# Attention on one core: one PSUM bank for the V product, a ring of three for plain scores and turned maxima, reciprocals and last divisions later

## The chip, the cores and the metric

The kernel runs on one core of a Trainium2 chip. The core has TensorE (PE in the profile, with its weight loads as PEld), VectorE (DVE), ScalarE (ACT), GpSimd (POOL) and a queue that issues DMAs (SP). TensorE writes into PSUM, eight banks of 512 float32 columns on 128 partitions; ScalarE and VectorE read it there. The metric is the device time of one execution in microseconds, median of the runs. The time before is 2050.35 us.

## The reference

One transformer layer on 2048 tokens of width 512, in float32: layer norm, causal attention with 16 heads of 32, an output projection, and a gated feed-forward part whose weights are packed in 4 bits.

```python
qkv = jnp.einsum('bsh,oh->bso', hidden_states, w_qkv)      # 16 heads of 32
scores = jnp.einsum('bhqd,bhkd->bhqk', q, k) * scale
scores = jnp.where(causal, scores, jnp.finfo(scores.dtype).min)
probs = jax.nn.softmax(scores, axis=-1)
attn = jnp.einsum('bhqk,bhkd->bhqd', probs, v)
...
x = x + attention(xn) + feed_forward(xn)
```

## The kernel before

Three stages follow each other: norm and projection, attention, then output projection and feed-forward. Only `attention` is changed. It works on 8 pairs of heads (`p`, heads `a` = 0 and 1).

**What a pair needs.** The queries are four chunks of 512 (`qc`), the keys 16 tiles of 128 (`kt`). A *step* is one chunk with one key tile; the causal mask leaves 4, 8, 12 and 16 of them for the four chunks, 40 in a pair, 320 in all (`STEPS`, `NS`). On the four last tiles of a chunk, the diagonal ones, a step is 512, 384, 256 and 128 columns wide and gets a mask added by a small matmul.

- `scores_t` (L664, mask L669) makes the transposed scores of a step for both heads in `p_st`. The negative row maximum of each query is part of the product: it lies in three rows of `q_stack`.
- ACT takes the exponential of both heads in one instruction, `exps` (L536), into `e_sb`.
- `product_v` (L689) adds a step's product with V into `p_o`, with the sum of the exponentials in an extra column of V. When a chunk is complete, ACT copies it to `o_sb` (`copy_out`, L544) and SP stores it. The sums go through memory and come back as `compact`; `invert_sums` (L592) on DVE inverts them, and POOL multiplies the finished rows later (`normalise`). In the last pair, DVE divides at once from `p_o` (`divide`, L600 and L604).

**Where the row maxima come from.** Plain scores are made one *unit* at a time: `scores` (L634, one matmul of up to 512 columns into `p_s`) and `unit_max` on DVE (L579, on the diagonal L575). There are 80 units in a pair, some 12 groups ahead of their use. When the units of chunk `r` are through, DVE joins them (`join_parts`, L586), POOL splits the maxima into three bfloat16 parts (`split`, L492 to L502), PE turns them into rows (`turn_max`, L651, four matmuls of 128 columns for a head) and ACT copies the rows into `q_stack` (`max_row`, L528). A *turn* here is `turn_max` and its copy for one head.

**Buffers.** `p_st` has two buffers of two banks. `p_s` has two banks in turn: a unit waits until the maximum of the unit two before it is taken (`maxed`). `p_o` has two banks, chunk by chunk, and the turns use partitions 96 to 127 of the same banks.

**Order.** Each engine has its own written-out program, and semaphores join them. A *group* is two steps (`d`, in the changed kernel `k`; 20 in a pair, 160 in all). In a group PE issues: a quarter of the group's units, `scores_t` of the step two ahead, a quarter of the units, `scores_t` of the next one, a quarter, the first head's turn if one is due, `product_v` of both steps, the second head's turn, the last quarter. A group has 6 units at first, 4 from the twelfth on, and none after group 147. ACT does in a group: `copy_out` if a chunk has ended, both exponentials, then the copies of the turns.

## Time and profile before

| | |
|---|---|
| median of 3 runs | 2050.35 us (2049.04 to 2053.05) |
| the profiled execution | 2050.79 us, its span 2049.0 us |
| PE, DVE, ACT, POOL busy | 93%, 54%, 33%, 15% of the span |
| attention | from about 190 to 899.6 us |
| one pair of heads in the middle of attention | about 82 us |

The span is the time from the first to the last instruction; the execution's own time is 1.8 us longer. PE's busy time counts modelled ends of pipelined matmuls, so a busy PE can still be late; the starts of its instructions tell more.

### The profile page before, as it was taken

The page shows a single profiled execution, that of the slowest core. Times are in us where ns is not written, and L with a number is a line of the kernel's source. Part 1 is how long each engine was busy: PE and PEld are TensorE (multiplying, and loading weights), DVE is VectorE, ACT ScalarE, POOL GpSimd, SP SyncE. Part 2 cuts the span into 40 slices and gives each one's busy share as a digit, 9 for nine tenths or more (in the row PEclk, how much of TensorE's full clock was granted, in tenths as well). Part 3 has the DMA queues.
Part 4 walks back from the last instruction along what each step waited for, and adds up shares of the span by engine and source line. Part 5 has one row for each costly group of instructions (what it writes and reads, how often), then busy time and mean ns, then how long its engine had stood idle before and what let it go on. Part 6 is the DMA issues. An engine that isn't in the chain of part 4 may idle for free.

```text
span 2049.0 us, 23233 instructions
## 1 busy us (share of the span) xinstructions
PE 1908.9 (93%) x8448; PEld 1316.4 (64%) x8448; DVE 1098.8 (54%) x1703; ACT 681.7 (33%) x789; POOL 310.2 (15%) x339
## 2 busy tenths in 40 slices
PE   2996899999999999889999999999999999999998
PEld 2785344444444444335777778777877787778776
DVE  7220565555565565533555655655655565556553
ACT  2221244544545455321222222223223223222221
POOL 0002100100110101100222222222122212221221
PEclk9998799999999999999999999999999999999999
DMA  3654504134043040033101110111011101110002
GB/s 143 236 185 129 109 6 91 33 65 85 10 91 76 22 91 6 12 121 124 34 10 31 31 26 4 31 31 31 0 31 31 31 0 31 31 31 0 1 0 83
DMA packets 88852, 109.27 MB, mean 53 GB/s; under 512 B 44248, under 2 KB 60632, under 8 KB 85008
## 3 DMA queue, kind: packets, MB, share of 16 engines
q1 hardware_dynamic: 88784, 108.39, 19.6%
q8 instruction: 40, 0.66, 0.1%
q14 instruction: 28, 0.23, 0.0%
HBM read 75.09 MB, written 29.59 MB: 51 GB/s over the span
## 4 chain that ended last, share of the span: by engine, by line
DVE 21%; ACT 11%; POOL 10%; issue 7%; PE 6%; POOLq 0%; DVEq 0%; ACTq 0%
POOL poly L910 7%; DVE acc L983 5%; DVE inter L963 4%; DVE inter L967 4%; ACT inter L882 3%; POOL poly L907 3%; ACT gate L878 3%; ACT poly L879 3%; DVE weight L952 3%; ACT i_hi L885 2%; DVE magnitude L946 2%; DVE pair L939 2%; PE p_out L1048 1%; DVE high L943 1%; DVE pair L937 1%
## 5 line engine op out<-in xcount | busy, mean ns | idle before, releaser
L536 ACT ACTIVATE e_sb<-p_st 128x1024 f32<-128x1024 f32 (+1 forms) x320 | 278.7, 896 | 276.7 <-PE p_st L664 156.1
L579 DVE TENSOR_REDUCE max_part<-p_s 128x1 f32<-128x512 f32 x384 | 256.1, 687 | 124.8 <-PE p_s L634 122.6
L634 PE MATMUL p_s<-k_stack,q_stack 96*128 96x512 f32 (+3 forms) x640 | 251.9, 434 | 56.0 <-DVE max_part L579 25.1
L689 PE MATMUL p_o<-e_sb,v_stack 128*33 128x512 f32 (+5 forms) x1280 | 271.0, 545 | 0.0
L963 DVE SCALAR_TENSOR_TENSOR inter<-inter,gate 128x1024 f32<-128x1024 f32 x64 | 78.4, 1226 | 329.6 <-ACT inter L882 329.6
L634 PEld LDWEIGHTS p_s<-k_stack,q_stack 96*128 96x128 f32 x640 | 111.3, 192 | 198.3 <-issue 93.5
L48 PE MATMUL p_up<-xn_hi,w_hi 128*128 128x512 f32 x512 | 201.1, 393 | 25.5 <-DVE inter L967 25.5
L907 POOL TENSOR_SCALAR poly<-poly 128x1024 f32<-128x1024 f32 x64 | 67.5, 1054 | 930.6 <-ACT poly L879 930.6
L48 PE MATMUL p_out<-i_hi,w_hi 128*128 128x512 f32 x512 | 200.5, 392 | 3.1 <-DVE acc L983 3.1
L48 PE MATMUL p_gate<-xn_hi,w_hi 128*128 128x512 f32 x512 | 201.5, 394 | 0.7 <-ACT poly L879 0.7
L575 DVE CUSTOM_DVE_ANT_0 masked_scores<-p_s,score_mask 128x128 f32<-128x128 f32 (+3 forms) x256 | 124.2, 490 | 145.0 <-PE p_s L634 142.2
L49 PE MATMUL p_out<-i_lo,w_hi 128*128 128x512 f32 x512 | 200.3, 391 | 0.0
L50 PE MATMUL p_out<-i_hi,w_lo 128*128 128x512 f32 x512 | 200.1, 391 | 0.0
L50 PE MATMUL p_gate<-xn_hi,w_lo 128*128 128x512 f32 x512 | 199.4, 389 | 0.0
L50 PE MATMUL p_up<-xn_hi,w_lo 128*128 128x512 f32 x512 | 199.3, 389 | 0.0
L49 PE MATMUL p_up<-xn_lo,w_hi 128*128 128x512 f32 x512 | 199.3, 389 | 0.0
L49 PE MATMUL p_gate<-xn_lo,w_hi 128*128 128x512 f32 x512 | 199.3, 389 | 0.0
L664 PE MATMUL p_st<-q_stack,k_stack 128*128 128x512 f32 (+3 forms) x640 | 185.6, 373 | 1.8 <-ACT q_stack L528 0.7
L872 ACT ACTIVATE w_hi<-weight 128x1024 fp32r<-128x1024 f32 x48 | 51.0, 1062 | 387.1 <-DVE weight L952 387.1
L910 POOL TENSOR_TENSOR poly<-poly,gate 128x1024 f32<-128x1024 f32 x64 | 153.2, 2394 | 5.3
L983 DVE TENSOR_TENSOR acc<-acc,p_out 128x2048 f32<-128x2048 f32 x64 | 146.0, 2281 | 8.7 <-PE p_out L50 8.7
L882 ACT ACTIVATE inter<-poly 128x1024 f32<-128x1024 f32 x64 | 68.0, 1062 | 240.6 <-POOL poly L910 240.6
(101 smaller groups left out, 2520.4 us busy)
## 6 DMA issues: line engine op xcount, KB each, us to landing
q_stack<-qk_scratch SPq DMA_DIRECT2D x48, 256.0 KB, 7.2
k_stack<-qk_scratch SPq DMA_DIRECT2D x48, 256.0 KB, 8.6
qk_scratch<-out_hi SPq DMA_DIRECT2D x32, 256.0 KB, 2.6
qk_scratch<-out_lo SPq DMA_DIRECT2D x32, 256.0 KB, 3.3
scales<-in_gate_up_s SPq DMA_DIRECT2D x128, 64.0 KB, 2.4
x_sb<-in_x SPq DMA_DIRECT2D x4, 1024.0 KB, 11.8
xn_lo_scratch<-xn_lo_made SPq DMA_DIRECT2D x1, 4096.0 KB, 13.3
v_scratch<-out_v SPq DMA_DIRECT2D x16, 256.0 KB, 2.0
```

Of the source, the lines that this page charges most:

```text
L48: nc.tensor.matmul(out, w_hi, x_hi, start=first, stop=False)
L49: nc.tensor.matmul(out, w_hi, x_lo, start=False, stop=False)
L50: return nc.tensor.matmul(out, w_lo, x_hi, start=False, stop=last)
L536: nc.scalar.activation(e_sb[:, g % E_BUFS, :, 0:w], p_st[:, g % 2, :, 0:w], ACT.Exp, scale=SCALE).then_inc(exp_done, 1)
L579: nc.vector.reduce_max(part, p_s[:, n % 2, 0:w], AX.X).then_inc(maxed, 1)
L634: nc.tensor.matmul(p_s[:, n % 2, 0:w], q_stack[p % PB][a][0:ROWS, i * P:(i + 1) * P], k_stack[p % PB][a][0:ROWS, b * W:b * W + w], start=T ...
L664: last = nc.tensor.matmul(p_st[:, g % 2, a, 0:W - q0], k_stack[p % PB][a][:, kt * P:(kt + 1) * P], q_stack[p % PB][a][:, qc * W + q0:(qc + ...
L689: last = nc.tensor.matmul(p_o[a * VW:a * VW + width, qc % 2, q0:], v_stack[p % PB][:, kt, a, 0:width], e_sb[:, g % E_BUFS, a, 0:W - q0], s ...
L882: nc.scalar.activation(inter[:, :, :], poly[:, :, :], ACT.Tanh, scale=GELU_B).then_inc(tanh_done, 1)
L910: nc.gpsimd.tensor_tensor(poly[:, :, :], poly[:, :, :], gate[:, :, :], ALU.mult).then_inc(poly_done, 1)
L963: nc.vector.scalar_tensor_tensor(inter[:, :, :], inter[:, :, :], 1.0, gate[:, :, :], ALU.add, ALU.mult).then_inc(gelu_done, 1)
L983: nc.vector.tensor_tensor(here, here, p_out[:, :, :], ALU.add).then_inc(added, 1)
```

## The change

- `p_o` has one bank. `product_v` at the start of a chunk waits until ACT has copied the chunk before it.
- `p_s` has three banks, used in turn by units and by turns (`ring`, `slot`). `bank_free` waits for the user three places before: for its maximum, if that was a unit, for ACT's copy `max_row`, if it was a turn.
- Both heads' turns of a chunk stand at the head of one group on PE, and their copies stand between the group's two exponentials on ACT.
- `invert_sums` stands at step 16 of a pair instead of step 8, and POOL's `normalise` moves with it. SP stores the first chunk of a pair before it sends the reciprocals.
- In the last pair all chunks but the last are copied out by ACT, and DVE divides them from `o_sb`, at steps 20, 24 and 28, after the last unit.

`GS` is 2 and `PIECES` is 1, so steps, groups and units are as before, and so are the instructions of `scores_t`, `exps` and `product_v`.

```diff
-    LEAD = 2
+    S_BUFS = 3
...
+    TURN_LEAD = 2
+    FIRST_LEAD = 1
...
-            BATCHES[doubles_with_batch(p, r)].append((p, r))
+            last = p * NU + UNITS_TO[r]
+            BATCHES[-1 if last <= FIRST else next(k for k in range(NG) if unit_end[k] >= last)].append((p, r))
+            wanted = (p * NS + CHUNK_START[r] - LEAD) // GS
             for a in range(2):
-                first = p * NS + CHUNK_START[r] - LEAD
-                due = first // 2 - 1
-                if r < 2:
-                    due = p * NS // 2 - 4 + r
-                TURNS[max(-1, due)].append((p, r, a))
+                TURNS[max(-1, -1 if p == 0 and r < 2 else wanted - (FIRST_LEAD if p == 0 else TURN_LEAD))].append((p, r, a))
...
+    ring = list(range(FIRST)) + TURNS[-1]
+    for k in range(NG):
+        ring += TURNS[k] + units_of(k)
+    slot = {what: n for n, what in enumerate(ring)}
...
-        p_st = ctx.enter_context(nc.psum_tensor("p_st", [P, 2, 2, W], F32))
-        p_s = ctx.enter_context(nc.psum_tensor("p_s", [P, 2, W], F32))
-        p_o = ctx.enter_context(nc.psum_tensor("p_o", [P, 2, W], F32))
+        p_st = ctx.enter_context(nc.psum_tensor("p_st", [P, ST_BUFS, PH, W], F32))
+        p_s = ctx.enter_context(nc.psum_tensor("p_s", [P, S_BUFS, W], F32))
+        p_o = ctx.enter_context(nc.psum_tensor("p_o", [P, W], F32))
...
                     store_chunk(p - 1, TC - 1)
                     load_sums(p - 1)
+                if p < PAIRS - 1:
+                    store_chunk(p, 0)
+                if p > 0:
                     load_reciprocals(p - 1)
                 if p < PAIRS - 1:
-                    for qc in range(TC - 1):
+                    for qc in range(1, TC - 1):
                         store_chunk(p, qc)
...
-                p, s = divmod(2 * d, NS)
-                if p > 0 and s in (14, 16, 26, 28):
+                p, s = divmod(GS * k, NS)
+                if p > 0 and s in (24, 28, 32, 36):
                     normalise(p - 1, products % TC, splits)
                     products += 1
...
             for t in TURNS[-1]:
                 max_row(*t)
-            for g in range(LEAD):
-                exps(g)
-            for d in range(ND):
-                p, s = divmod(2 * d - 1, NS)
-                if d and s in CHUNK_END:
-                    if p < PAIRS - 1:
-                        copy_out(p, CHUNK_END[s])
-                for g in (2 * d + LEAD, 2 * d + LEAD + 1):
-                    if g < NSTEP:
-                        exps(g)
-                for t in TURNS[d]:
+            for x in range(LEAD * PIECES):
+                exps(x)
+            for k in range(NG):
+                x = (GS * k + LEAD) * PIECES
+                copy_out_before(k)
+                exps(x)
+                for t in TURNS[k]:
                     max_row(*t)
+                exps(x + 1)
...
-                p = PAIRS - 1
-                dve.wait_ge(pv_done, p * NS + CHUNK_START[qc] + 4 * (qc + 1))
-                if qc:
-                    dve.wait_ge(divided, 2 * qc)
-                nc.vector.reciprocal(recip[:, :], p_o[:, qc % 2, :]).then_inc(inverted, 1)
-                dve.wait_ge(inverted, qc + 1)
+                p, c = PAIRS - 1, (PAIRS - 1) * TC + qc
+                dve.wait_ge(o_copied, c + 1)
+                for a in range(2):
+                    rows, sums = slice(2 * a * D, 2 * a * D + D), slice(2 * a * D + D, 2 * a * D + VW)
+                    if qc:
+                        dve.wait_ge(divided, 2 * qc)
+                    nc.vector.reciprocal(recip[rows, :], o_sb[sums, c % 2, :]).then_inc(inverted, 1)
+                for a in range(2):
+                    rows = slice(2 * a * D, 2 * a * D + D)
+                    dve.wait_ge(inverted, 2 * qc + a + 1)
+                    nc.vector.tensor_tensor(attn_rows(p, a, qc), o_sb[rows, c % 2, :], recip[rows, :],
+                                            ALU.mult).then_inc(divided, 1)
...
-            for d in range(ND):
-                p, s = divmod(2 * d - 1, NS)
-                if p == PAIRS - 1 and s in CHUNK_END:
-                    divide(CHUNK_END[s])
-                if p and s == 7:
+            for k in range(NG):
+                p, s = divmod(GS * k, NS)
+                if p and s == 16:
                     invert_sums(p - 1)
-                for n in units_of(d):
+                for n in units_of(k):
                     unit_max(n)
-                for p, r in BATCHES[d]:
-                    join_parts(p, r)
-            divide(TC - 1)
+                for p_, r in BATCHES[k]:
+                    join_parts(p_, r)
+                if p == PAIRS - 1 and s in (20, 24, 28):
+                    divide({20: 0, 24: 1, 28: 2}[s])
+            divide_last()
...
+            def bank_free(n):
+
+                before = ring[n - S_BUFS] if n >= S_BUFS else None
+                if before in turn_index:
+                    pe.wait_ge(max_rows, turn_index[before] + 1)
+                elif before is not None:
+                    pe.wait_ge(maxed, before + 1)
...
             def turn_max(p, r, a):
 
+                n = slot[p, r, a]
                 pe.wait_ge(max_split, p * TC + r + 1)
-                if r < 2:
-                    if p:
-                        pe.wait_ge(o_copied, (p - 1) * TC + 3)
-                elif p < PAIRS - 1:
-                    pe.wait_ge(o_copied, p * TC + r - 1)
-                else:
-                    pe.wait_ge(divided, 2 * (r - 1))
-                if turn_index[p, r, a]:
-                    pe.wait_ge(max_rows, turn_index[p, r, a])
+                bank_free(n)
                 for t in range(W // P):
-                    last = nc.tensor.matmul(p_o[ROWS:P, turn_bank(r), t * P:(t + 1) * P],
+                    last = nc.tensor.matmul(p_s[ROWS:P, n % S_BUFS, t * P:(t + 1) * P],
                                             max_cols[:, a, 4 * r + t, :], ident[:, :], start=True, stop=True)
                 last.then_inc(max_turned, 1)
...
-                if kt == 0:
-                    pe.wait_ge(max_rows, max(i for t, i in turn_index.items() if t[0] == p and t[1] <= max(1, qc)) + 1)
-                    if c >= 2:
-                        if p < PAIRS - 1 or qc < 2:
-                            pe.wait_ge(o_copied, c - 1)
-                        else:
-                            pe.wait_ge(divided, 2 * (qc - 1))
-                pe.wait_ge(exp_done, g + 1)
+                if kt == 0 and p * TC + qc:
+                    pe.wait_ge(o_copied, p * TC + qc)
+                pe.wait_ge(exp_done, (g + 1) * PIECES)
...
-            pe.wait_ge(o_cleared, 1)
             for t in TURNS[-1]:
                 turn_max(*t)
             pe.wait_ge(filled, NF)
...
+                for t in TURNS[k]:
                     turn_max(*t)
-                for g in (2 * d, 2 * d + 1):
+                some_units(0, 4)
+                scores_t(x)
+                some_units(1, 4)
+                scores_t(x + 1)
+                some_units(2, 4)
+                for g in range(GS * k, GS * k + GS):
                     product_v(g)
-                for t in TURNS[d][1::2]:
-                    turn_max(*t)
-                for n in spread[3]:
-                    scores(n)
+                some_units(3, 4)
```

PE's program around one turn, in the third pair, before. `p_s<-k_stack` is a unit, `p_s<-ident_bf` or `p_o<-ident_bf` a turn, `p_st<-q_stack` is `scores_t`, `p_o<-e_sb` is `product_v`:

```order
L634 MATMUL p_s<-k_stack,q_stack 128x512 [waits maxed]
L664 MATMUL p_st<-q_stack,k_stack 128x384 [waits exp_done]
L664 MATMUL p_st<-q_stack,k_stack 128x384
L669 MATMUL p_st<-mask_k,ident_bf 128x128 x2
L634 MATMUL p_s<-k_stack,q_stack 128x512 [waits maxed]
L651 MATMUL p_o<-ident_bf,max_cols 32x128 [waits max_rows,o_copied,max_split]
L651 MATMUL p_o<-ident_bf,max_cols 32x128 x3
L689 MATMUL p_o<-e_sb,v_stack 33x512 [waits exp_done]
L689 MATMUL p_o<-e_sb,v_stack 33x512
L689 MATMUL p_o<-e_sb,v_stack 33x512 [waits exp_done]
L689 MATMUL p_o<-e_sb,v_stack 33x512
L651 MATMUL p_o<-ident_bf,max_cols 32x128 [waits max_rows,o_copied,max_split]
```

The same place on PE in the changed kernel:

```order
L684 MATMUL p_s<-ident_bf,max_cols 32x128 [waits maxed,max_split]
L684 MATMUL p_s<-ident_bf,max_cols 32x128 x3
L684 MATMUL p_s<-ident_bf,max_cols 32x128 [waits maxed,max_split]
L684 MATMUL p_s<-ident_bf,max_cols 32x128 x3
L674 MATMUL p_s<-k_stack,q_stack 128x512 [waits maxed]
L700 MATMUL p_st<-q_stack,k_stack 128x512 [waits exp_done]
L700 MATMUL p_st<-q_stack,k_stack 128x512
L706 MATMUL p_st<-mask_k,ident_bf 128x128 x2
L674 MATMUL p_s<-k_stack,q_stack 128x512 [waits max_rows]
L700 MATMUL p_st<-q_stack,k_stack 128x384 [waits exp_done]
L700 MATMUL p_st<-q_stack,k_stack 128x384
L706 MATMUL p_st<-mask_k,ident_bf 128x128 x2
```

The turns have moved from both sides of `product_v` to the head of the group, and the unit behind the first `scores_t` now waits for `max_rows`, which is ACT's copy of the first turn.

ACT's program in the same part of the changed kernel. `e_sb<-p_st` is an exponential, `q_stack<-p_s` the copy of a turn, `o_sb<-p_o` a `copy_out`:

```order
L551 ACTIVATE e_sb<-p_st 128x1024 [waits pv_done,st_ready] x11
L540 ACTIVATE q_stack<-p_s 32x512 [waits max_turned] x2
L551 ACTIVATE e_sb<-p_st 128x2x384 [waits pv_done,st_ready]
L551 ACTIVATE e_sb<-p_st 128x2x256 [waits pv_done,st_ready]
L551 ACTIVATE e_sb<-p_st 128x2x128 [waits pv_done,st_ready]
```

The copies stand behind the last of the eleven wide exponentials, that of the group's first step, where before they stood behind both exponentials of a group.

DVE's program in the last pair, before. `masked_scores` and `max_part` are units:

```order
L575 ISA masked_scores,max_part<-p_s,score_mask 128x128 [waits maxed,scored]
L575 ISA max_part 128x1
L600 RECIPROCAL recip<-p_o 128x512 [waits pv_done]
L604 TENSOR_TENSOR acc<-p_o,recip 32x512 [waits inverted]
L604 TENSOR_TENSOR acc<-p_o,recip 32x512
L579 TENSOR_REDUCE max_part<-p_s 128x1 [waits scored] x6
```

And in the changed kernel:

```order
L594 ISA masked_scores,max_part<-p_s,score_mask 128x512 [waits maxed,scored]
L594 ISA max_part 128x1
L605 TENSOR_REDUCE row_max<-max_part 128x2x4 [waits max_split,maxed]
L611 RECIPROCAL rcompact<-compact 128x32 [waits rsums_out,sums_loaded]
L621 RECIPROCAL recip<-o_sb 32x512 [waits o_copied]
L621 RECIPROCAL recip<-o_sb 32x512
L625 TENSOR_TENSOR acc<-o_sb,recip 32x512 [waits inverted] x2
```

The divisions stand behind the last unit and the last `row_max`; before, the units of later chunks stood behind them.

## Rows read from the trace of the kernel before

**Rows 1.** Waits of PE and PEld in attention (us in total, times, longest)

```profile
PE p_s L634 <- DVE max_part L579: 25.1, 30, 4.5
...
PEld p_s L634 <- DVE max_part L579: 58.8, 99, 4.9
...
PEld p_s L634 <- DVE max_part L575: 27.6, 73, 1.0
```

**Rows 2.** Timeline of PE in two ordinary groups (start us, us)

```profile
656.51 0.73 PE L634 MATMUL p_s<-k_stack,q_stack 96*128 96x512 f32 x2
657.08 0.63 PE L664 MATMUL p_st<-q_stack,k_stack 128*128 128x512 f32 x2
657.79 0.50 PE L634 MATMUL p_s<-k_stack,q_stack 96*128 96x512 f32 x1
658.13 0.63 PE L664 MATMUL p_st<-q_stack,k_stack 128*128 128x512 f32 x2
...
659.97 0.64 PE L664 MATMUL p_st<-q_stack,k_stack 128*128 128x512 f32 x2
660.45 0.40 PE L634 MATMUL p_s<-k_stack,q_stack 96*128 96x512 f32 x1
660.69 0.64 PE L664 MATMUL p_st<-q_stack,k_stack 128*128 128x512 f32 x2
```

**Rows 3.** Timeline of DVE in the first of these groups

```profile
657.04 1.98 DVE L579 TENSOR_REDUCE max_part<-p_s 128x1 f32<-128x512 f32 x3 [1.37 <-PE p_s L634]
```

**Rows 4.** Timeline of PE at the reciprocals: first, second and last pair

```profile
342.79 0.53 PE L634 MATMUL p_s<-k_stack,q_stack 96*128 96x512 f32 x1 [1.80 <-DVE max_part L579]
...
343.79 3.05 PE L689 MATMUL p_o<-e_sb,v_stack 128*33 128x512 f32 x8
...
426.45 0.49 PE L634 MATMUL p_s<-k_stack,q_stack 96*128 96x512 f32 x1 [2.34 <-DVE max_part L579]
...
752.55 0.49 PE L634 MATMUL p_s<-k_stack,q_stack 96*128 96x512 f32 x1 [0.94 <-DVE max_part L579]
...
753.30 1.70 PE L689 MATMUL p_o<-e_sb,v_stack 128*33 128x512 f32 x8
```

**Rows 5.** Busy time of PE, PEld, DVE, ACT, POOL; PEclk, DMA share, GB/s

```profile
830.00:835.00 5.00, 5.00 (x15) 1.84 (x12) 1.35 (x3) 0.00 (x0) 0.00 (x0) 0.53 0.00 0
```

**Rows 6.** Timeline of PE and DVE at the first division of the last pair

```profile
828.72 0.79 PE L634 MATMUL p_s<-k_stack,q_stack 96*128 96x512 f32 x1 [4.35 <-DVE max_part L579]
...
823.15 3.35 DVE L600 RECIPROCAL recip<-p_o 128x512 f32<-128x512 f32 x1
```

**Rows 7.** Timeline of PE in a group with a turn

```profile
395.08 0.40 PE L651 MATMUL p_o<-ident_bf,max_cols 128*32 128x128 bf16 x4
395.41 0.62 PE L634 MATMUL p_s<-k_stack,q_stack 96*128 96x256 f32 x2
395.87 0.62 PE L664 MATMUL p_st<-q_stack,k_stack 128*128 128x512 f32 x2
...
396.42 0.48 PE L634 MATMUL p_s<-k_stack,q_stack 96*128 96x512 f32 x1
```

**Rows 8.** Timeline of ACT in that group; ns min/median/max of exponentials and of copies

```profile
396.65 1.73 ACT L536 ACTIVATE e_sb<-p_st 128x1024 f32<-128x1024 f32 x2 [0.54 <-PE p_st L669]
...
L536 ACT ACTIVATE e_sb<-p_st x320: 377/1024/1029, 229.6 to 892.1; 128x1024 f32<-128x1024 f32 x128, 128x512 f32<-128x512 f32 x32
...
L528 ACT ACTIVATE q_stack<-p_o x64: 590/591/593, 223.6 to 869.8; 32x512 fp32r<-32x512 f32 x64
L544 ACT ACTIVATE o_sb<-p_o x28: 591/599/605, 238.5 to 815.5; 97x512 f32<-97x512 f32 x28
```

**Rows 9.** Timeline of DVE and POOL from a chunk's last unit to its split

```profile
299.54 0.69 DVE L575 CUSTOM_DVE_ANT_0 masked_scores<-p_s,score_mask 128x512 f32<-128x512 f32 x1 [1.57 <-PE p_s L634]
...
301.65 0.22 POOL L502 CAST max_cols<-rest 128x8 bf16<-128x8 f32 x1
```

**Rows 10.** Timeline of PE at the start of attention

```profile
224.38 0.58 PE L651 MATMUL p_o<-ident_bf,max_cols 128*32 128x128 bf16 x4 [0.77 <-ACT q_stack L528]
```

More of the change, by code:

```diff
@@ L270, in attention @@
     ONE = D + 1
+    GS = 2
+    LEAD = 2
+    PH = 2
+    ST_BUFS = 2
     E_BUFS = 4
-    LEAD = 2
+    S_BUFS = 3
+    UNITS_GROUP = 4
+    UNITS_FIRST = 6
+    UNITS_AHEAD = 48
+    TURN_LEAD = 2
+    FIRST_LEAD = 1
     STEPS = [(qc, kt, max(0, kt * P - qc * W)) for qc in range(TC) for kt in range(4 * qc + 4)]
@@ L514, in _ @@
             splits = products = 0
-            for d in range(-1, ND):
-                for p, r in BATCHES[d]:
+            for k in range(-1, NG):
+                for p, r in BATCHES[k]:
                     split(p, r, products)
                     splits += 1
-                p, s = divmod(2 * d, NS)
-                if p > 0 and s in (14, 16, 26, 28):
+                p, s = divmod(GS * k, NS)
+                if p > 0 and s in (24, 28, 32, 36):
                     normalise(p - 1, products % TC, splits)
@@ L527, in max_row, with exps @@
                 act.wait_ge(max_turned, turn_index[p, r, a] + 1)
-                nc.scalar.activation(q_stack[p % PB][a][ROWS:P, r * W:(r + 1) * W], p_o[ROWS:P, turn_bank(r), :],
-                                     ACT.Copy).then_inc(max_rows, 1)
-            def exps(g):
+                nc.scalar.activation(q_stack[p % PB][a][ROWS:P, r * W:(r + 1) * W],
+                                     p_s[ROWS:P, slot[p, r, a] % S_BUFS, :], ACT.Copy).then_inc(max_rows, 1)
+            def exps(x):
+                g, heads = piece(x)
+                if g >= NSTEP:
+                    return
                 w = W - STEPS[g % NS][2]
-                act.wait_ge(st_ready, g + 1)
-                if g >= E_BUFS:
-                    act.wait_ge(pv_done, g - E_BUFS + 1)
-                nc.scalar.activation(e_sb[:, g % E_BUFS, :, 0:w], p_st[:, g % 2, :, 0:w], ACT.Exp,
+                act.wait_ge(st_ready, x + 1)
+                if x >= E_BUFS:
+                    act.wait_ge(pv_done, piece(x - E_BUFS)[0] + 1)
+                nc.scalar.activation(e_sb[:, x % E_BUFS, :, 0:w], p_st[:, x % ST_BUFS, :, 0:w], ACT.Exp,
                                      scale=SCALE).then_inc(exp_done, 1)
@@ L631, in scores @@
                     pe.wait_ge(qk_loaded[p % PB][a], 96 * (p // PB + 1))
-                if n >= 2:
-                    pe.wait_ge(maxed, n - 1)
-                nc.tensor.matmul(p_s[:, n % 2, 0:w], q_stack[p % PB][a][0:ROWS, i * P:(i + 1) * P],
+                bank_free(slot[n])
+                nc.tensor.matmul(p_s[:, slot[n] % S_BUFS, 0:w], q_stack[p % PB][a][0:ROWS, i * P:(i + 1) * P],
                                  k_stack[p % PB][a][0:ROWS, b * W:b * W + w], start=True, stop=True
@@ L659, in scores_t @@
                 if kt == 0:
-                    pe.wait_ge(max_rows, turn_index[p, qc, 1] + 1)
-                if g >= 2:
-                    pe.wait_ge(exp_done, g - 1)
-                for a in range(2):
-                    last = nc.tensor.matmul(p_st[:, g % 2, a, 0:W - q0], k_stack[p % PB][a][:, kt * P:(kt + 1) * P],
+                    pe.wait_ge(max_rows, turn_index[p, qc, heads[-1]] + 1)
+                if x >= ST_BUFS:
+                    pe.wait_ge(exp_done, x - ST_BUFS + 1)
+                for n, a in enumerate(heads):
+                    last = nc.tensor.matmul(p_st[:, x % ST_BUFS, n, 0:W - q0],
+                                            k_stack[p % PB][a][:, kt * P:(kt + 1) * P],
                                             q_stack[p % PB][a][:, qc * W + q0:(qc + 1) * W], start=True,
-                                        stop=not DIAG[s])
+                                            stop=not DIAG[s])
                 if DIAG[s]:
-                    for a in range(2):
-                        last = nc.tensor.matmul(p_st[:, g % 2, a, 0:P], ident[:, :], mask_k[:, :], start=False,
+                    for n, a in enumerate(heads):
+                        last = nc.tensor.matmul(p_st[:, x % ST_BUFS, n, 0:P], ident[:, :], mask_k[:, :], start=False,
                                                 stop=True)
```

90 lines of the change are left out of this document (49 added, 41 removed).

## The prediction

> **What bounds the kernel now.** I read the waits of PE first, then its timeline group by group, because PE sets the pace of attention. DVE, ACT and POOL wait for it and it waits for them only briefly. In the table of waits the unit matmuls stand out: their weight loads wait 58.8 + 27.6 us for DVE's maxima, 172 times, and PE itself is idle for 25.1 us because of them [rows 1]. This is the ring of two. The timeline shows it. In the group at 656.51, the unit behind the first `scores_t` starts 0.71 us after it (657.08, 657.79), and the next `scores_t` 0.34 us later. In the group behind it, where a narrow unit left DVE early, the same starts are 0.48 and 0.24 apart [rows 2]. So a late maximum costs 0.33 us: 0.23 on the unit and 0.10 on the `scores_t` whose weights could not be loaded early.
>
> DVE also stalls PE in a coarser way. Once in each of pairs one to six it waits for the sums to come back through memory, its queue of maxima stands, and PE is idle: 1.80 us the first time, 2.34 the second, 0.94 the last [rows 4]. I count six, 9.8 us together. Twice the clock fell too: after the first stall the product took 3.05 us, after the last the same product of another pair took 1.70, so one fall costs 1.35 us [rows 4]. The longest stalls were not the ones that brought a fall. [...]
>
> **What the change removes.** The sum is made against the profiled execution, 2050.8 us, 0.4 above the median of the runs.
>
> - *Ring of three.* In an ordinary group a unit then waits for the maximum of the unit three before. At each place of the written order that one is behind `product_v` or one `scores_t` further back, and DVE, busy little over half the time, is done. Of the 172 waits, six are the reciprocals, two the divisions, some 15 the 24 first units, where DVE is the limit anyway. About 148 at 0.33 are 48 us. The ends: from PE's idle time alone 25.1 − 9.8 − 8.8 = 6.5 us; from the weight loads 86.4 less about 20 for the same places, 66 us. I take 48, because the 0.33 is read from starts and the two tables count less and more than the delay.
> - *Reciprocals at step 16.* The sums came back in the middle of the second to fourth group at the latest; now they have four groups more. The stalls go: 9.8 + 2 falls × 1.35 = 12.5 us. Four groups of 4 us cover it; without them the 12.5 stay.
> - *Last divisions.* They cost DVE two reciprocals and two multiplications each, about 8 us instead of 4.8, but stand behind the last unit, where nothing on PE waits for DVE. The next chunk waits for ACT's copy instead. Gone are two stalls of 4.35 and about 4.4, the slow clock behind them (5 us at 0.53 instead of 1 is 2.4; the second I count at 1.2) and 0.7 where `scores_t` waits for a turn: 13 us. The last chunk's end is as before.
> - *Start.* The four first turns wait for each other, 0.77 us three times [rows 10]; with three banks most of that goes, and the first units run a little closer. 3 us, between 0 and 4.
>
> Together 76.5 us. The single `p_o` bank I cost at nothing: a copy takes 0.599 us [rows 8], ACT does it first in the next group, and PE has at least four matmuls for `scores_t` and mostly three units before the next product, 1.5 to 2 us. Without that cover it would be some 0.7 us at each of 31 chunk ends, 22 us. [...]
>
> **What the change adds.** The turns now take places in the ring. After the two turns of a group come one unit, `scores_t`, and then a unit whose bank is the first turn's. It waits for ACT's copy, and on ACT this copy stands behind the exponential of the very `scores_t` that was just issued. So PE is idle for an exponential and a copy. From the start of `scores_t` (395.87): the exponential starts at 396.65, 0.78 later [rows 7, 8]; it takes 1.03 with its gap, the copy 0.59 [rows 8], the next matmul another 0.1: 2.50. Without the wait the unit starts at 396.42, 0.55 later [rows 7]. The stall is 1.95 us. Every such group has a full-width first step, so this is the case each time.
>
> The unit between turns and `scores_t` also waits: for the last unit before the turns. DVE starts on a unit 0.53 after its matmul (656.51, 657.04) [rows 2, 3], is done 0.61 to 0.69 later, so the bank is free at about 1.28, where the unit could start at three times 0.33 = 1.0 (turn and unit are 0.33 apart at 395.08) [rows 7]. That is 0.3 us at full width, 0.25 on average. In all 2.2 us in each of 27 groups (four in each of pairs two to eight, less the one behind the last unit): 59.4 us.
>
> In the first pair two more turn groups follow at once on the group that makes the last units of their chunk. There PE waits for the maximum, the join and POOL's five splitting steps, 2.33 us from 299.54 to 301.87 [rows 9], plus the matmul's 0.5 and the units in the queue before it: about 3.2 and 2.4, and then the stall above with a narrower exponential, 1.65 each. 8.9 us.
>
> **The clock.** Each of these 29 groups has 1.7 to 3 us without a matmul, and around the stall stand turns of 128 columns and single units, so that PE streams little for longer than the stall. Of the six stalls at the reciprocals two brought a fall, of the two long ones both. These stalls are in sparser surroundings than the six, in denser than the two. I take 7 in 10, 20 falls of 1.35: 27 us; the ends are a third and all of them, 13 and 39 us.
>
> The sum is 2050.8 − 76.5 + 59.4 + 8.9 + 27 = 2069.6. [...]
>
> **The rivals.**
> - *The clock holds.* The turns' stalls are short, and stalls of 2.3 us before passed without a fall. With none the sum is 2042.6, faster by 0.4%. It decides in this direction up to 2 falls; from 9 on the kernel is slower. With 3 to 8, or with the same shift from the ring, the time is within 0.2%.
> - *The ring gives less, or all falls come.* If only half of the 48 us is real, since the delays partly overlap other loads, the time is 2094; with all falls 2082.
> - *The single bank of `p_o` is waited for.* ACT's copy comes late because the turn copies and exponentials stand before it. 22 us more, 2092. Against it: no turn stands in a group in front of a chunk end except at the last chunk, and there exponential and copies end before the products do.
> - *The change does nothing.* It would need the ring's waits to be hidden and the turn's stall to be hidden too. The stall can't be: the order of ACT and PE fixes it.
>
> **How the numbers follow.** The forecast, stalls of the turns with half to nearly all falls, 2056 to 2080: 0.58. Above that, with a smaller gain of the ring or all falls or a waited copy: 0.13. The clock holds or falls rarely and the ring gives all, under 2046: 0.19. Between: 0.10. A measurement of this kernel tells about 0.2%, 4 us, from no change. So slower 0.71, same 0.10, faster 0.19. The time I give is 2068, a little under the sum, because a fall that lies partly inside a stall costs less than 1.35. The range of 8 in 10 is 2043 to 2088.
>
> **What the profile of the changed kernel would show.** Ordinary groups: the unit 0.48 and the next `scores_t` 0.24 behind, no wait for `max_part`. Turn groups: PE's unit waits for `q_stack`, 1.9 us, about 27 times, and that row is the longest of PE's waits in attention. No stall at the `rcompact` reciprocals and no gap in the last pair until its end. A pair in the middle takes 82 − 5.6 − 2 + 9 + 5 = 88 us. PEclk in attention under 0.96. I am wrong if the stall is much shorter than 1.9, or if the clock stays at 1.0 through the turns.

## The result, and the profile after

The changed kernel takes 2074.23 us (median of 4 runs, 2073.13 to 2080.29). The kernel before takes 2050.23 us beside it (2049.04 to 2053.05). The ratio is 1.0121, with a 95% interval from 1.0099 to 1.0143: slower by 1.2%, 24 us. The profiled execution is the slowest of the four, 2080.29 us with a span of 2078.5, so its sums run up to 6 us above the median.

The page of the changed kernel, busy time and two lines of the slices:

```profile
span 2078.5 us, 23236 instructions
...
PE 1918.0 (92%) x8448; PEld 1336.6 (64%) x8448; DVE 1098.9 (53%) x1706; ACT 676.4 (33%) x792; POOL 310.2 (15%) x339
...
PE   2996898989989899889999999999999999999998
...
PEclk9998698999999999999999999999999999999999
```

The shares of the engines are almost those of before, so the page alone hides the cause. The waits of PE and PEld in attention (200 to 930 us; us in total, times, longest) tell it; they answer to [rows 1]:

```profile
PE p_s L674 <- ACT q_stack L540: 49.2, 29, 1.7
...
PE p_s L684 <- POOL max_cols L514: 6.6, 3, 2.8
PE p_s L674 <- DVE max_part L598: 4.1, 17, 0.3
...
PEld p_s L674 <- DVE max_part L598: 29.0, 54, 0.8
PEld p_s L674 <- DVE max_part L594: 14.3, 39, 0.8
...
PEld p_o L721 <- ACT o_sb L562: 0.4, 1, 0.4
```

The waits for maxima have halved on the weight loads (86.4 to 43.3 us) and are nearly gone on PE. Before, PE had a second such row beside the one in [rows 1], for the maxima on the diagonal:

```profile
PE p_s L634 <- DVE max_part L575: 7.4, 26, 0.6
```

So it is 32.5 us before and 4.1 after. The last row shown above is all that the product waits for the single `p_o` bank: once, 0.4 us, on a weight load. In place of the waits for maxima, PE stands idle 29 times, 49.2 us, for ACT's copy of a turn. An ordinary group in PE's timeline answers to [rows 2]:

```profile
308.85 0.74 PE L674 MATMUL p_s<-k_stack,q_stack 96*128 96x512 f32 x2
309.43 0.63 PE L700 MATMUL p_st<-q_stack,k_stack 128*128 128x512 f32 x2
309.90 0.40 PE L674 MATMUL p_s<-k_stack,q_stack 96*128 96x512 f32 x1
310.13 0.63 PE L700 MATMUL p_st<-q_stack,k_stack 128*128 128x512 f32 x2
```

The unit starts 0.47 us behind `scores_t` and the next `scores_t` 0.23 behind it: the undelayed case. Two turn groups of the same timeline. The first is followed by a fall of the clock, the second is not:

```profile
434.99 0.63 PE L700 MATMUL p_st<-q_stack,k_stack 128*128 128x512 f32 x2
...
437.48 0.79 PE L674 MATMUL p_s<-k_stack,q_stack 96*128 96x512 f32 x1 [1.73 <-ACT q_stack L540]
...
439.40 2.59 PE L721 MATMUL p_o<-e_sb,v_stack 128*33 128x512 f32 x8
...
490.76 1.91 PE L721 MATMUL p_o<-e_sb,v_stack 128*33 128x512 f32 x8
...
493.85 0.62 PE L700 MATMUL p_st<-q_stack,k_stack 128*128 128x512 f32 x2
...
496.33 0.50 PE L674 MATMUL p_s<-k_stack,q_stack 96*128 96x512 f32 x1 [1.73 <-ACT q_stack L540]
...
497.53 1.05 PE L721 MATMUL p_o<-e_sb,v_stack 128*33 128x512 f32 x4
```

From `scores_t` to the unit that waits for the copy it is 2.49 and 2.48 us. Behind the first stall the work up to the product takes 1.92 (437.48 to 439.40) where the second takes 1.20, and a product of eight matmuls takes 2.59 instead of 1.91. That fall cost at least 1.4 us; it is somewhat more, because the unit in front of the first product is narrower (256 columns) than the one in front of the second (512). ACT's timeline at the first of the two shows why PE waits:

```profile
435.79 1.02 ACT L551 ACTIVATE e_sb<-p_st 128x1024 f32<-128x1024 f32 x1 [3.14 <-PE p_st L706]
436.83 1.07 ACT L540 ACTIVATE q_stack<-p_s 32x512 fp32r<-32x512 f32 x2
```

ACT had been idle for 3.14 us, for the last 1.4 of them with both turns done on PE (their last matmul ends at 434.42), and then did the exponential first. The first copy ends at about 437.4 and PE's unit starts at 437.48.

Busy time by stretch of the changed kernel, from its first `product_v` to its first matmul of the output projection, and of one pair (PE, PEld, DVE, ACT, POOL, PEclk, DMA share, GB/s):

```profile
228.80:930.20 701.40, 637.41 (x3013) 313.85 (x3012) 385.18 (x905) 321.33 (x407) 68.00 (x178) 0.93 0.21 44
431.50:517.00 85.50, 78.13 (x385) 39.07 (x384) 46.25 (x118) 40.81 (x53) 9.36 (x24) 0.96 0.27 57
```

and the same stretch of the kernel before:

```profile
232.80:899.60 666.80, 624.60 (x3013) 293.73 (x3012) 383.57 (x903) 326.18 (x404) 67.83 (x178) 0.99 0.22 45
```

The stretch grew by 34.6 us although it began 4.0 earlier; from its end to the end of the span it is 1148.3 us, against 1149.4 before. Two stretches of the changed kernel in which the clock is low, the slow start of attention and one fall:

```profile
191.64:232.60 40.96, 23.74 (x71) 13.40 (x72) 15.09 (x47) 6.20 (x9) 19.42 (x24) 0.50 0.96 202
...
696.81:703.64 6.83, 6.63 (x18) 2.91 (x18) 1.65 (x6) 1.44 (x3) 0.00 (x0) 0.50 0.09 23
```

It is 0.50 in both. A granted clock of 0.93 over 701.4 us is then 98 us at 0.50 (with a share x at 0.50, 1 − x/2 = 0.93). The slow parts of the two stretches of attention, added up from the traces, are 101 us (4 of them the end of the slow start) and 17 us. So 84 us more ran at 0.50, which is some 42 us of work lost.

### The profile page after: what moved, and what is told of

Its sections match the earlier page's. It is cut to its first block, busy times and chain, and to the rows that moved or that the text cites. A ratio compares the mean times of both kernels' runs of the same rounds, so it can differ in the third digit from the quotient of the medians.

```text
span 2078.5 us, 23236 instructions
## 1 busy us (share of the span) xinstructions
PE 1918.0 (92%) x8448; PEld 1336.6 (64%) x8448; DVE 1098.9 (53%) x1706; ACT 676.4 (33%) x792; POOL 310.2 (15%) x339
## 4 chain that ended last, share of the span: by engine, by line
DVE 21%; ACT 11%; POOL 10%; issue 6%; PE 6%; POOLq 0%; DVEq 0%; ACTq 0%
POOL poly L943 7%; DVE acc L1016 5%; DVE inter L996 4%; DVE inter L1000 4%; ACT inter L915 3%; POOL poly L940 3%; ACT gate L911 3%; ACT poly L912 3%; DVE weight L985 3%; ACT i_hi L918 2%; DVE magnitude L979 2%; DVE pair L972 2%; PE p_out L1081 1%; DVE high L976 1%; PE p_gate L1081 1%
## 5 line engine op out<-in xcount | busy, mean ns | idle before, releaser
L598 DVE TENSOR_REDUCE max_part<-p_s 128x1 f32<-128x512 f32 x384 | 250.6, 686 | 167.4 <-PE p_s L674 166.3
L674 PE MATMUL p_s<-k_stack,q_stack 96*128 96x512 f32 (+3 forms) x640 | 258.2, 444 | 73.5 <-ACT q_stack L540 49.2
L721 PE MATMUL p_o<-e_sb,v_stack 128*33 128x512 f32 (+5 forms) x1280 | 291.9, 580 | 0.0
L674 PEld LDWEIGHTS p_s<-k_stack,q_stack 96*128 96x128 f32 x640 | 120.0, 204 | 209.4 <-issue 93.9
L721 PEld LDWEIGHTS p_o<-e_sb,v_stack 128*33 128x33 f32 (+1 forms) x1280 | 66.6, 119 | 143.7 <-issue 94.7
```

The costliest lines, as they stand in the source:

```text
L598: nc.vector.reduce_max(part, p_s[:, slot[n] % S_BUFS, 0:w], AX.X).then_inc(maxed, 1)
L674: nc.tensor.matmul(p_s[:, slot[n] % S_BUFS, 0:w], q_stack[p % PB][a][0:ROWS, i * P:(i + 1) * P], k_stack[p % PB][a][0:ROWS, b * W:b * W + ...
L721: last = nc.tensor.matmul(p_o[a * VW:a * VW + width, q0:], v_stack[p % PB][:, kt, a, 0:width], e_sb[:, x % E_BUFS, a if PH == 2 else 0, 0: ...
```

## The experiments

Two questions were open: what the turns' stall costs by itself and through the clock, and what each other part gives. My theory was that of the prediction: everything but the turns' place is a gain, and the copy behind the dependent exponential costs idle time and falls. The rivals: the clock has nothing to do with it, or the single `p_o` bank is waited for. The kernel before took 2050.09 us beside `copy_first`, `turns_before_v`, `turns_before_v_two` and `late_recips`, and 2051.61 beside `filler`, `copy_split` and `late_both`. Intervals of the ratios are about 0.2% to either side, so a difference between two medians is known to some 4 us.

### Copies ahead of the exponential: `copy_first`

```diff
                 copy_out_before(k)
+                for t in TURNS[k]:
+                    max_row(*t)
                 exps(x)
-                for t in TURNS[k]:
-                    max_row(*t)
                 exps(x + 1)
```

> The changed kernel, but ACT copies the turns at the head of the group, before the exponential of the group's first step. Theory (the stall is an exponential and a copy that stand on ACT behind scores_t, 1.9 us at 29 groups, and brings the falls of the clock): PE's wait for q_stack, 49.2 us, goes to under 3, PEclk in attention rises from 0.93 to 0.98 or more, and the time falls by 56 us of stalls and about 25 of clock to 1990 to 2003. Rival (the turns themselves cost, by taking two of three ring places, wherever their copy stands): the wait moves to max_part, and the time stays above 2040.

Measured: 1984.23 us, ratio 0.9676 (0.9655 to 0.9698). PE's waits in attention of this kernel:

```profile
PE p_s L684 <- POOL max_cols L514: 6.6, 3, 2.8
...
PE p_s L674 <- DVE max_part L598: 4.1, 17, 0.3
```

The row with `q_stack` is gone and the other two are as in the changed kernel. Its stretch of attention:

```profile
228.70:835.40 606.70, 591.96 (x3014) 298.91 (x3013) 383.66 (x905) 318.20 (x408) 67.97 (x178) 0.99 0.24 50
```

Two moved lines on ACT are worth 90 us, of which the trace of the changed kernel shows only 49.2 as idle. The remaining 41 need another cause, and PEclk went from 0.93 to 0.99.

### The stall kept, but filled with matmuls: `filler`

Behind the first `scores_t` of 29 turn groups, PE does 28 matmuls of 128 columns into the bank of the first turn. They are additional work whose results nothing uses.

```diff
                 scores_t(x)
+                if TURNS[k] and units:
+                    for _ in range(28):
+                        nc.tensor.matmul(p_s[0:D, slot[TURNS[k][0]] % S_BUFS, 0:P], ident[:, 0:D], ident[:, :],
+                                         start=True, stop=True)
                 some_units(1, 4)
```

> The changed kernel with 28 matmuls of 128 columns (identity into the idle quadrant of the first turn's bank, results unused) behind the first scores_t of each of the 29 turn groups, some 1.5 us of work inside a stall of 1.9. It leaves the wait for ACT's copy as it is and only keeps PE busy. Theory (the stalls cost twice, 56 us idle and some 40 us by the clock that falls behind them): PE's idle time becomes small, PEclk in attention rises to 0.98 or more, the time falls to 2028 to 2045. Rival (the clock has little part in it, the wait is all): 2068 to 2080.

Measured: 2035.21 us, ratio 0.9928 (0.9913 to 0.9942). PE's timeline in one such group, and a stretch of attention, of this kernel:

```profile
474.65 0.62 PE L700 MATMUL p_st<-q_stack,k_stack 128*128 128x512 f32 x2
...
475.33 1.74 PE L749 MATMUL p_s<-ident_bf 128*32 128x128 bf16 x28
477.12 0.50 PE L674 MATMUL p_s<-k_stack,q_stack 96*128 96x512 f32 x1
...
233.00:840.00 607.00, 596.20 (x3601) 324.03 (x3600) 343.47 (x866) 294.59 (x375) 61.32 (x169) 1.00 0.24 49
```

The same stretch of the changed kernel:

```profile
233.00:840.00 607.00, 554.24 (x2610) 274.33 (x2610) 325.73 (x824) 277.90 (x351) 60.30 (x164) 0.93 0.23 49
```

The unit still comes 2.47 us behind `scores_t`, so the wait is unchanged. Only PE is busy in it, the granted clock is 1.00, and the kernel is 39.0 us faster. This takes the two costs apart: 39.0 us are the clock (2074.2 − 2035.2), 51.0 the delay itself (2035.2 − 1984.2). The rival without the clock would have had this kernel at 2074.

The two traces also tell which stalls the clock followed. The stretches below run from the unit behind one stall to the unit behind a later one. First the changed kernel, then the same three stretches of `filler`:

```profile
410.86:437.48 26.62, 22.70 (x129) 11.99 (x129) 14.90 (x31) 12.66 (x19) 1.06 (x5) 1.00 0.72 144
437.48:463.10 25.62, 23.89 (x113) 11.89 (x113) 13.45 (x37) 12.12 (x16) 1.06 (x5) 0.94 0.14 33
522.94:550.12 27.18, 25.45 (x113) 12.41 (x113) 13.62 (x37) 12.12 (x16) 1.07 (x5) 0.88 0.14 31
...
394.81:421.42 26.61, 26.02 (x184) 15.10 (x185) 14.89 (x31) 12.65 (x19) 1.06 (x5) 1.00 0.71 144
421.42:445.50 24.08, 24.02 (x141) 12.80 (x141) 13.40 (x37) 12.12 (x16) 1.06 (x5) 1.00 0.16 35
503.73:527.84 24.11, 24.05 (x140) 12.80 (x140) 13.40 (x37) 12.12 (x16) 1.06 (x5) 1.00 0.13 36
```

The first stretch holds two stalls, and after neither did the clock fall: both kernels take 26.6 us. The second is 1.5 us longer in the changed kernel, the third 3.1. The table has the same for all 29 stalls: the time from the unit behind a stall to the unit behind the next (from the last one to 924.55, where the last matmul of attention starts, 883.44 in `filler`), and the stretch in which the granted clock is low.

| pair, chunk | unit at | us, changed kernel | us, `filler` | difference | clock low from, for |
|---|---|---|---|---|---|
| 1, 2 | 250.36 | 33.70 | 32.36 | 1.34 | 249.66, 6.83 |
| 1, 3 | 284.06 | 32.33 | 29.71 | 2.62 | 283.80, 6.83 |
| 2, 0 | 316.39 | 12.19 | 10.56 | 1.63 | 317.93, 3.41 |
| 2, 1 | 328.58 | 20.56 | 16.05 | 4.51 | 328.17, 10.24 |
| 2, 2 | 349.14 | 27.05 | 24.11 | 2.94 | 348.65, 6.83 |
| 2, 3 | 376.19 | 34.67 | 31.60 | 3.07 | 375.96, 6.83 |
| 3, 0 | 410.86 | 10.56 | 10.56 | 0.00 | none |
| 3, 1 | 421.42 | 16.06 | 16.05 | 0.01 | none |
| 3, 2 | 437.48 | 25.62 | 24.08 | 1.54 | 437.40, 3.41 |
| 3, 3 | 463.10 | 33.23 | 31.62 | 1.61 | 464.70, 3.41 |
| 4, 0 | 496.33 | 10.56 | 10.56 | 0.00 | none |
| 4, 1 | 506.89 | 16.05 | 16.05 | 0.00 | none |
| 4, 2 | 522.94 | 27.18 | 24.11 | 3.07 | 522.73, 6.83 |
| 4, 3 | 550.12 | 33.11 | 31.63 | 1.48 | 550.04, 3.41 |
| 5, 0 | 583.23 | 12.19 | 10.56 | 1.63 | 584.17, 3.41 |
| 5, 1 | 595.42 | 16.06 | 16.06 | 0.00 | none |
| 5, 2 | 611.48 | 25.66 | 24.07 | 1.59 | 611.48, 3.41 |
| 5, 3 | 637.14 | 33.25 | 31.63 | 1.62 | 638.78, 3.41 |
| 6, 0 | 670.39 | 10.57 | 10.56 | 0.01 | none |
| 6, 1 | 680.96 | 16.05 | 16.05 | 0.00 | none |
| 6, 2 | 697.01 | 27.18 | 24.11 | 3.07 | 696.81, 6.83 |
| 6, 3 | 724.19 | 33.14 | 31.59 | 1.55 | 724.12, 3.41 |
| 7, 0 | 757.33 | 12.19 | 10.57 | 1.62 | 758.25, 3.41 |
| 7, 1 | 769.52 | 16.06 | 16.05 | 0.01 | none |
| 7, 2 | 785.58 | 25.66 | 24.08 | 1.58 | 785.56, 3.41 |
| 7, 3 | 811.24 | 33.25 | 31.62 | 1.63 | 812.86, 3.41 |
| 8, 0 | 844.49 | 10.57 | 10.56 | 0.01 | none |
| 8, 1 | 855.06 | 16.13 | 16.13 | 0.00 | none |
| 8, 2 | 871.19 | 53.36 | 50.33 | 3.03 | 870.89, 6.83 |

The granted clock is 0.50 in each of these stretches. Three of them, one of each length:

```profile
328.17:338.41 10.24, 9.83 (x34) 5.06 (x34) 4.25 (x9) 3.22 (x6) 1.06 (x5) 0.50 1.01 208
...
437.40:440.81 3.41, 3.33 (x10) 1.68 (x12) 1.13 (x3) 1.32 (x3) 0.00 (x0) 0.50 0.19 45
...
522.73:529.56 6.83, 6.62 (x18) 2.90 (x18) 1.64 (x6) 1.45 (x3) 0.00 (x0) 0.50 0.09 22
```

`filler` has one such stretch between its first stall and the end of attention:

```profile
280.08:283.49 3.41, 3.41 (x30) 3.21 (x27) 0.09 (x2) 1.55 (x3) 0.00 (x0) 0.50 0.00 0
```

So there are 19 falls. In 11 of them the clock was low for 3.4 us, and each of these cost 1.5 or 1.6 us; in the other eight it was low for 6.8 or 10.2 us, and they cost 1.3 to 4.5 (the 1.3 where `filler` has its own fall, at 280.08). The ten stretches behind stalls without a fall are equal within 0.01 us. From the first stall on, the profiled executions differ by 41.2 us in attention, all of it in stretches with a fall. Two of the 19 lie in the first pair, where the clock falls in `copy_first` too (246.60 and 280.70, shown below).

### One copy ahead of the exponential: `copy_split`

```diff
                 copy_out_before(k)
+                for t in TURNS[k][0::2]:
+                    max_row(*t)
                 exps(x)
-                for t in TURNS[k]:
+                for t in TURNS[k][1::2]:
                     max_row(*t)
```

> The changed kernel, but ACT copies the first head's turn before the exponential of the group's first step and the second head's after it. Then the first unit's bank is free in time, and only the next unit, one scores_t later, waits for the exponential and a copy. Theory (the wait is the distance in the ring against ACT's order): the stall shrinks from 1.9 to about 1.0 us, 27 us of idle time, and the time lies between the two variants, at 2010 to 2030 with fewer falls of the clock. Rival (any one copy behind the exponential costs the full stall): over 2060; or the second wait is covered: under 1990.

Measured: 2019.42 us, ratio 0.985 (0.9836 to 0.9863). The waits of PE and the stretch:

```profile
PE p_s L676 <- ACT q_stack L540: 28.3, 29, 1.1
...
290.00:866.00 576.00, 542.53 (x2769) 272.59 (x2768) 344.54 (x805) 300.50 (x378) 64.85 (x163) 1.00 0.25 52
```

The stall has moved to the second turn's bank and is 1.0 us on average instead of 1.7. It costs 35.2 us against `copy_first`, that is 1.2 for each of 29, nearly all of it the delay. From the second pair on none of these stalls brought a fall: the granted clock of that stretch is 1.00, where the changed kernel has 0.93 between the same two times. The price of a stall is not proportional to its length here: 1.2 us for 1.0 us of idle time, against 3.1 (90 / 29) for 1.7.

### Turns just before `product_v`: `turns_before_v`

The turns stand behind three quarters of the group's units, the ring follows that order, and the copies stand behind both exponentials, as they did before.

```diff
-        ring += TURNS[k] + units_of(k)
+        most = 3 * len(units_of(k)) // 4
+        ring += units_of(k)[:most] + TURNS[k] + units_of(k)[most:]
...
-                for t in TURNS[k]:
-                    turn_max(*t)
                 some_units(0, 4)
...
                 some_units(2, 4)
+                for t in TURNS[k]:
+                    turn_max(*t)
                 for g in range(GS * k, GS * k + GS):
                     product_v(g)
...
                 exps(x)
+                exps(x + 1)
                 for t in TURNS[k]:
                     max_row(*t)
-                exps(x + 1)
```

> The changed kernel, but both turns stand right before product_v on PE, and ACT copies them after both exponentials, as in the kernel before; the ring's order follows. Theory: as with the copies first, and the two waits for POOL's split in the first pair (6.6 us) go too: 1982 to 1996, some 5 to 9 us under the variant with the copies first. Rival (the place of the turns doesn't matter, only ACT's order): the same time as that variant within 3 us.

Measured: 1965.78 us, ratio 0.9596 (0.9575 to 0.9617). It beats both kernels, by 4.0% and 5.2%, and is 18.5 us faster than `copy_first`, where I had expected 5 to 9. In its timeline of PE the product now lies behind the turns and covers the copies:

```profile
453.32 0.48 PE L675 MATMUL p_s<-k_stack,q_stack 96*128 96x512 f32 x1
453.73 0.64 PE L685 MATMUL p_s<-ident_bf,max_cols 128*32 128x128 bf16 x8
454.29 0.85 PE L722 MATMUL p_o<-e_sb,v_stack 128*33 128x256 f32 x8
```

PE's waits in attention of this kernel:

```profile
PE p_s L685 <- POOL max_cols L515: 2.3, 3, 1.6
...
PE p_s L675 <- DVE max_part L599: 0.9, 3, 0.3
```

Two stretches of `copy_first`, both in its first pair:

```profile
246.60:253.40 6.80, 6.80 (x25) 3.22 (x22) 2.67 (x4) 2.05 (x4) 0.00 (x0) 0.50 0.00 0
280.70:284.10 3.40, 3.40 (x14) 1.12 (x12) 1.48 (x6) 0.49 (x2) 0.00 (x0) 0.50 0.00 0
```

Most of the 18.5 (20.3 between the two profiled executions) can be placed. Counted by the starts of `scores_t`, `turns_before_v` is 10.8 us ahead after the two turn groups of the second pair and gains another 1.35 in each pair behind, 0.34 for a turn group. In the first pair POOL's splits are waited for 4.3 us less (they have the group's units as cover), and the two stretches above, 10.2 us at 0.50 and fully busy, cost about 5; in `turns_before_v` the granted clock is 1.00 from 233 to 816.

### The same with a ring of two: `turns_before_v_two`

```diff
-    S_BUFS = 3
+    S_BUFS = 2
```

> As the variant with the turns before product_v, but with a ring of two banks. Measures the third bank alone. Theory (a late maximum costs 0.33 us, about 148 times, and the second turn of a group waits another 0.4 for its bank): 45 to 60 us slower than with three banks. Rival (the ring's waits were mostly covered; PE's idle time alone is what it can give back, 6.5 us): under 20 us slower.

Measured: 2033.73 us, ratio 0.9923 (0.9903 to 0.9943), 68.0 us more than with three banks. In its waits PE now stands before units and before turns:

```profile
PE p_s L675 <- DVE max_part L595: 7.4, 26, 0.6
PE p_s L685 <- DVE max_part L595: 6.7, 16, 0.5
PE p_s L675 <- DVE max_part L599: 6.3, 21, 0.6
...
PE p_s L685 <- DVE max_part L599: 4.7, 16, 0.4
```

11.4 of the 68 are waits of turns for a bank, a cost that neither the kernel before nor the changed one pays. That leaves 57 for the units, by subtraction.

### The reciprocals alone: `late_recips`

This is the kernel before, with its `invert_sums` at step 16, POOL's `normalise` behind it, and the first chunk stored before the reciprocals are sent.

```diff
+                if p < PAIRS - 1:
+                    store_chunk(p, 0)
+                if p > 0:
                     load_reciprocals(p - 1)
...
-                if p > 0 and s in (14, 16, 26, 28):
+                if p > 0 and s in (24, 28, 32, 36):
...
-                if p and s == 7:
+                if p and s == 15:
                     invert_sums(p - 1)
```

> The kernel before with one part of the change: reciprocals at step 16, normalise and the store of the first chunk moved with them. Theory: the six stalls and two falls go, 12.5 us: 2036 to 2040. Rival (the reciprocals then hold up something later, or the stall hid other waits): within 4 us of 2050.

Measured: 2036.64 us, ratio 0.9941 (0.992 to 0.9962), 13.5 us faster than before. Its longest wait for a maximum is the last pair's division, which it keeps:

```profile
PE p_s L637 <- DVE max_part L582: 15.1, 23, 4.5
```

Against [rows 1] this row is 10.0 us shorter; my count of the six stalls was 9.8.

### Reciprocals and last divisions: `late_both`

On top of `late_recips`, the last pair's chunks are copied out and divided from `o_sb` at steps 20, 24 and 28, behind the units, as in the changed kernel. Two `p_o` banks, a ring of two and the turns' old place stay.

```diff
-                if p == PAIRS - 1 and s in CHUNK_END:
-                    divide(CHUNK_END[s])
...
+                if p == PAIRS - 1 and s in (20, 24, 28):
+                    divide({20: 0, 24: 1, 28: 2}[s])
-            divide(TC - 1)
+            divide_last()
```

> The kernel before with its ring of two and two banks for p_o, reciprocals at step 16 and the last pair's divisions copied out by ACT and done behind the last unit. Theory: another 13 us under the variant with late reciprocals alone (2036.6): 2021 to 2026. Rival (the division's stalls hid other waits, or the two 32-partition reciprocals of each chunk delay the end): within 4 us of 2036.

Measured: 2022.54 us, ratio 0.9863 (0.9847 to 0.988), 14.1 us less than `late_recips`. Its waits for maxima are short ones only, those of the ring of two:

```profile
PE p_s L653 <- DVE max_part L580: 7.2, 26, 0.6
PE p_s L653 <- DVE max_part L584: 6.3, 21, 0.6
```

These are the unit rows of `turns_before_v_two` again. The two kernels differ in the turns' bank and in the number of `p_o` banks. The difference of their times is 11.2 us, and the turns' own waits are 11.4, so within the error of 4 us nothing is left for the single `p_o` bank.

## Why the prediction came out as it did

The kernels can be put in a line: before 2050.1, `late_recips` 2036.6, `late_both` 2022.5, `turns_before_v` 1965.8, `copy_first` 1984.2, `filler` 2035.2, changed kernel 2074.2. The steps add up by construction; each is good to some 4 us. They are not all single edits: from `late_both` to `turns_before_v` the ring, the turns' bank and the number of `p_o` banks change together. Beside them the terms of the prediction's sum:

| term | forecast | measured |
|---|---|---|
| reciprocals at step 16 | −12.5 | −13.5 |
| last divisions behind the units | −13 | −14.1 |
| ring of three, start, single `p_o` bank | −51 (48 + 3 + 0) | −56.8 |
| turns at the head: unit behind them, POOL's split | +12.4 (27 × 0.25, 3.2 + 2.4) | +18.5 |
| copy behind the exponential, delay | +56 (27 × 1.95, 2 × 1.65) | +51.0 |
| the clock | +27 | +39.0 |
| together | +18.9 | +24.1 |

- **The ring.** The forecast spacing of ordinary groups, 0.48 and 0.24, came as 0.47 and 0.23. The ring is worth somewhat more than 148 delays of 0.33. Of the two tables that bounded it, the one of the weight loads (66 us) was the nearer. The bound from PE's idle time (6.5) left out the row for the maxima on the diagonal, 7.4 us; even with it, 13.9, most of the gain is missed, since most of a late start lies under the modelled end of the matmul before: in [rows 2] the unit at 657.79 is 0.23 us late, and 0.08 of that lies behind the end of `scores_t` (657.08 + 0.63).
- **Reciprocals and divisions.** Both as forecast, and each was run by itself. The changed kernel has no stall at `rcompact`, and in the last pair all divisions but the last stand behind the last unit. The 4.35 us and the 0.53 in the 13 us of the divisions are those of [rows 6] and [rows 5]; the second stall, estimated at 4.4, is 4.46 in the trace of before, and the clock is at 0.50 for 3.41 us there (from 851.72), which is 1.7 us lost where I had 1.2. These are DVE's rows in the changed kernel:

```profile
892.99 6.72 DVE L621 RECIPROCAL recip<-o_sb 32x512 f32<-32x512 f32 x2
...
924.87 3.36 DVE L633 RECIPROCAL recip<-p_o 128x512 f32<-128x512 f32 x1 [5.84 <-PE p_o L721]
```

- **The single `p_o` bank.** Costed at nothing, and that is what was found: the product waits for the copy once, 0.4 us, and `late_both` against `turns_before_v_two` leaves 0.2 us, inside the error. In `p_s` a third bank gave 57 us; in `p_o` the second gave nothing that shows, since the copy has other PE work as cover.
- **The stall.** Forecast 2.50 us from `scores_t` to the unit, found 2.48 and 2.49; forecast 27 full ones and two in the first pair, found 29 waits, the longest row of PE's waits in attention, as said. I had 1.9 us for that row's length where it shows 1.7, since it counts idle time and not the distance between starts. By the starts of `scores_t` in `filler` and `copy_first`, each full stall delayed what follows by 1.93 us, where 1.95 was forecast.
- **The turns at the head.** Forecast 12.4, measured 18.5. The waits for POOL's split sum to 6.6 us over three, forecast 5.6 over two. The unit behind the turns cost 0.34 us a group instead of 0.25. The rest is the clock: in `copy_first` it falls twice in the first pair, about 5 us, which the sum had among the falls of the stalls.
- **The clock.** This is the term that was furthest off, 27 us against 39.0. That these stalls bring falls was right (with them filled, attention is 41.2 us shorter), and so was the number: I took 20, the trace has 19. Their price was wrong. I had 1.35 us from one product that was slow for a part of a fall. By the same [rows 4] the unit and the turn before that product were slow too: from 342.79 to 343.79 it is 1.00 us, from 752.55 to 753.30 only 0.75, which makes 1.6. And I took every fall to be as short as that one, while in 8 of 19 the clock stayed low two or three times as long. Measured are 2.1 us for a fall (39.0 / 19; by the traces 41.2 / 19).
- **Where the clock fell.** That 20 falls came so near was partly luck, as 7 in 10 was set between two of six and two of two. The 29 stalls are not alike in it, though all 27 of the later pairs are 1.73 us long:

| turns of | stalls | with a fall |
|---|---|---|
| first pair, chunks 2 and 3 | 2 | 2 |
| second pair, all chunks | 4 | 4 |
| pairs three to eight, chunk 0 | 6 | 2 |
| the same, chunk 1 | 6 | 0 |
| the same, chunk 2 | 6 | 6 |
| the same, chunk 3 | 5 | 5 |

- **What decides.** That stays open. I had argued from the narrow work around the stall, but the eight turn matmuls and the single unit stand in front of all 29. Chunk 0 shows that the written order alone doesn't settle it: the groups at 410.86 and 583.23 do the same work, and only the second brought a fall. The granted clock of attention is 0.93, where I said under 0.96. With falls in all 29 groups the sum would have come to 2082; the trace has ten of the 29 without one. That 29 × 1.35 also makes 39 is chance.
- **The sum.** It came within 6 us of the measured time because errors cancelled: ring, reciprocals, divisions and delay were together 13 us better than forecast, clock and turns' place 18 worse.
- **The rival that the clock holds** gave 2042.6. `filler`, where it does hold, took 2035.2.
- A mid pair took 85.5 us in the stretch shown and 86.9 to 87.2 in the four behind it, 88 forecast. In the stretch shown the clock was low for the shortest time of the five.

So the kernel is slower because ACT's copy of a turn stands behind the exponential while the turn stands at the head of the group. Of 90 us that it costs, the waits show 49; 84 us of gains in the other parts, less 18.5 for the turns' place, could not pay for it.

## What to carry to other kernels

When buffers of two kinds of work share a ring, look for the slowest release in it. Here a copy of 0.6 us stood behind an exponential whose input PE had only just issued, so in each of 29 groups PE waited for the whole way to ACT and back. Let the consumer that frees a bank go first, or put the producer where a long product follows. Price a stall of TensorE twice, once as delay and once by the clock (51 and 39 us here), and test the second part by filling the stall with matmuls nobody uses. Read the price of a fall over the whole time that the clock is low, and from more than one fall: here 1.35 us came from a part of one, and the mean was 2.1. Judge each part of a combined change by itself: the ring, the reciprocals and the divisions were good here, the turns' place was not, and a version that keeps the parts and mends the order is 5.2% faster than the change and 4.0% faster than what it started from.

## What the hardware showed unasked

- Stalls of 1.73 us (1.30 in the first pair), 29 times in attention, in a PE that was otherwise busy, brought the granted clock from 0.99 to 0.93 and cost 39 us beside 51 us of delay. With 1.0 us on average in the same places (`copy_split`) it was 1.00 from the second pair on, and with 28 small matmuls in them (`filler`) 1.00.
- These stalls, with nearly the same matmuls directly around them, brought a fall in 19 places and none in ten. Each fall left the clock at 0.50 for 3.4, 6.8 or 10.2 us.
- The filler matmuls, 128 columns and 32 output rows each, took 1.74 us for 28 and needed no data of their own. As a remedy they gave back 39 of 90 us; the order of two instructions on ACT gave back all 90.
